# One decoder layer on one core: the feed-forward weights made ternary during the self-attention, and the first cross-attention inputs fetched there

## The reference

```
x = x + self_attention(layernorm(x))      # 16 heads of 128, window of 128, rope, sink, grouped output in two matrices
x = x + cross_attention(layernorm(x))     # 16 query heads of 32, 4 key/value heads, 1024 context rows a batch
x = x + feed_forward(layernorm(x))
```

```python
def weight_quant(w):
    scale = 1.0 / jnp.clip(jnp.mean(jnp.abs(w)), EPS)
    return jnp.clip(jnp.round(w * scale), -1.0, 1.0) / scale
gate = bitlinear(x, w_gate); up = bitlinear(x, w_up)
intermediate = jax.nn.silu(gate) * up
return h_bitlinear(intermediate, w_down)   # a Walsh-Hadamard transform over 2048 before the rounding
```

## Time and profile before

| | |
|---|---|
| time before, median of 3 runs | 1869.34 us (1868.5 to 1874.75) |
| the profiled execution, its own time | 1871.28 us |
| its span in the trace | 1869.4 us |
| mean granted TensorE clock | 0.968 of full speed |
| busy share of the span | PE 89%, DVE 62%, ACT 65%, POOL 63% |
| self-attention, steps | from about 88 to 659 us |
| cross-attention | from 659 to 1494 us |
| feed-forward | from 1494 us to the end |

### The profile page before, as it was taken

One profiled execution on the slowest core, in us unless ns is written; L12 is line 12 of the kernel. 1 busy time (PEld: TensorE's weight loads), 2 busy tenths in 40 slices (PEclk: granted clock), 3 DMA queues, 4 the chain that ended last, 5 costly groups with the idle time before them and its releaser, 6 DMA issues. The chain is left out here.

```text
span 1869.4 us, 24714 instructions
## 1 busy us (share of the span) xinstructions
PE 1663.9 (89%) x8118; PEld 1161.0 (62%) x8118; DVE 1163.6 (62%) x1997; ACT 1213.6 (65%) x1979; POOL 1177.1 (63%) x1080
## 2 busy tenths in 40 slices
PE   6999999999999958999999999999999606999996
PEld 3588888888888735556555655566656302666664
DVE  2366666666766536666855576556757266677764
ACT  2366666656665524887876687667869344788775
POOL 0478777877877503675755576556757306888892
PEclk9999999999999978999999999999999958999999
DMA  6100000000000055112210311120100080010000
GB/s 215 46 12 12 13 20 16 12 12 24 12 7 12 6 171 138 31 26 76 57 43 26 88 31 40 32 49 18 43 23 23 29 315 0 12 35 27 31 18 24
DMA packets 47103, 85.40 MB, mean 46 GB/s; under 512 B 7548, under 2 KB 12028, under 8 KB 45952
## 3 DMA queue, kind: packets, MB, share of 16 engines
q1 hardware_dynamic: 45136, 82.67, 14.3%
q10 hardware_dynamic: 1840, 1.14, 0.2%
HBM read 52.26 MB, written 12.58 MB: 35 GB/s over the span
## 5 line engine op out<-in xcount | busy, mean ns | idle before, releaser
L1146 POOL TENSOR_TENSOR x_p_lo<-x_p,x_p_hi 128x1024 fp32r<-128x1024 f32 x192 | 455.4, 2384 | 300.2 <-ACT x_p_hi L980 299.5
L1095 DVE TENSOR_REDUCE x_maxes<-x_ps_a 128x1 f32<-128x1024 f32 x256 | 313.1, 1223 | 258.1 <-PE x_ps_a L1229 257.2
L958 ACT ACTIVATE x_p<-x_ps_b,x_any_valid 128x1024 f32<-128x1024 f32 x256 | 284.9, 1113 | 168.5 <-PE x_ps_b L1217 167.8
L1217 PE MATMUL x_ps_b<-x_Q,x_K 100*128 100x512 f32 x512 | 228.1, 526 | 3.7 <-ACT x_p L958 2.2
L980 ACT ACTIVATE x_p_hi<-x_p 128x1024 fp32r<-128x1024 f32 x192 | 203.1, 1058 | 4.8
L1229 PE MATMUL x_ps_a<-x_K,x_Q 99*128 99x512 f32 x512 | 166.3, 406 | 6.8 <-DMA x_Q<-x_p_lo 3.9
L1255 PE MATMUL x_ps_o<-x_p_hi,x_V 128*96 128x512 f32 x384 | 157.1, 409 | 1.2 <-POOL x_p_lo L1146 1.2
L1256 PE MATMUL x_ps_o<-x_p_lo,x_V 128*96 128x512 f32 x384 | 150.9, 393 | 0.0
L1217 PEld LDWEIGHTS x_ps_b<-x_Q,x_K 100*128 100x128 f32 x512 | 90.1, 191 | 97.3 <-issue 76.1
L331 ACT ACTIVATE a_work<-a_ps_s,a_neg_max,a_q_r 128x256 f32<-128x256 f32 (+1 forms) x256 | 134.0, 538 | 4.7 <-DVE a_neg_max L419 4.7
L1260 PE MATMUL x_ps_o<-x_p,x_V 128*96 128x512 f32 x256 | 120.4, 591 | 0.0
(11 more groups left out here) (256 smaller groups left out, 4300.9 us busy)
## 6 DMA issues: line engine op xcount, KB each, us to landing
a_w_raw<-in_L_attn_out_w SPq DMA_DIRECT2D x8, 1024.0 KB, 7.8
x_ctxT<-in_ctx SPq DMA_DIRECT2D x8, 1024.0 KB, 7.3
x_Q<-x_q_hi SPq DMA_DIRECT2D x104, 64.0 KB, 2.0
a_xt<-in_x SPq DMA_DIRECT2D x16, 256.0 KB, 2.8
x_scratch<-a_work SPq DMA_DIRECT2D x16, 256.0 KB, 2.0
x_xt<-x_scratch SPq DMA_DIRECT2D x16, 256.0 KB, 3.6
x_K<-x_k_hi SPq DMA_DIRECT2D x32, 128.0 KB, 2.3
x_x1t<-x_scratch SPq DMA_DIRECT2D x16, 256.0 KB, 3.0
```

The lines of the kernel that those rows point to most:

```text
L958: act.activation(p[:, r, :, :], ps_b[:, :, :], ACT.Exp, scale=any_valid[:, b % 2:b % 2 + 1]).then_inc(exp_ready, 1)
L1095: dve.tensor_reduce(out=maxes[:, h2, r, 3:4], in_=ps_a[:, :, :], axis=mybir.AxisListType.XY, op=ALU.max)\
L1146: pool.tensor_tensor(out=p_lo[:, r], in0=p[:, r], in1=p_hi[:, r].bitcast(F32), op=ALU.subtract).then_inc(lo_ready, 1)
L1217: last = pe.matmul(ps_b[:, j, :], K[0:ROWS + 4, g, kb * P:(kb + 1) * P], Q[0:ROWS + 4, hh, :], start=True, stop=True)
```

## The change

The rounding of the three feed-forward weights leaves the feed-forward. It is done in the self-attention, in 24 chunks of 128 x 1024 (8 for each weight), in two passes over the fp32 weights in DRAM:

- Steps c = 0 to 23: SP loads a chunk into one of four slots, and DVE sums its magnitudes (a `tensor_reduce` of 128 x 1024, placed between L437 and L439). After 8 chunks DVE adds up (steps 8, 16, 24); SP writes 128 sums to DRAM, waits, and loads them back to all partitions; DVE adds them and makes mean and reciprocal (steps 11, 19, 27).
- Steps c = 14 to 37: the chunk is loaded again; ACT rounds it (`Copy` with a scale, before the wait of L316) and clips it from one side as bf16 (`Relu`, between the four `Exp` and the sink's); in the next step DVE clips the other side (a `tensor_scalar` of bf16, 128 x 1024, ahead of L380); SP stores the chunk to `ffn_quant` in DRAM. The weights are stored with the opposite sign, and four scale factors change sign.
- A buffer `shared` of 128 x 9216 fp32 outlives the phases. It holds the raw output matrices first, then the chunks, from c = 42 on the context, `wk`, `wq`, `wv`, and from c = 57 the first four tiles of x1. The cross-attention does not load these any more.
- In the last batch of the cross-attention SP loads gate and up as bf16 (2 MB each) from `ffn_quant` over the context and query weights. Down is loaded at the start of the feed-forward, behind two tiles of x2. The feed-forward begins with a `Silu` of 128 x 1.

```diff
+            def load_abs(k):
+                if k == 0:
+                    sp.wait_ge(w12_made, H1)
+                if k >= 4:
+                    sp.wait_ge(f_part_ready, k - 3)
+                sp.dma_start(chunk_view(f_abs[:, k % 4, :], k), ffn_source(k)).then_inc(f_abs_in[k % 4], 16)
+            def load_raw(k):
+                if k >= 2:
+                    sp.wait_ge(f_clip_ready, k - 1)
+                sp.dma_start(chunk_view(f_raw[:, k % 2, :], k), ffn_source(k)).then_inc(f_raw_in[k % 2], 16)
+            def store_quant(k):
+                sp.wait_ge(f_quant_ready, k + 1)
+                sp.dma_start(ffn_quant[k // 8, :, k % 8 * 1024:(k % 8 + 1) * 1024], f_quant[:, k % 2, :]).then_inc(f_stored[k % 2], 16)
...
+            for c in range(STEPS + 3):
+                if c + 2 < FFN_CHUNKS:
+                    load_abs(c + 2)
+                if 0 <= c - 16 < FFN_CHUNKS:
+                    store_quant(c - 16)
+                if 0 <= c - 12 < FFN_CHUNKS:
+                    load_raw(c - 12)
+                if c in (9, 17, 25):
+                    exchange_sums(c // 8 - 1)
...
# ACT, in step c, ahead of qT_hi
+                if 0 <= c - 14 < FFN_CHUNKS:
+                    k = c - 14
+                    act.wait_ge(f_raw_in[k % 2], 16 * (k // 2 + 1))
+                    act.wait_ge(f_scale_ready, k // 8 + 1)
+                    act.activation(f_raw[:, k % 2, :], f_raw[:, k % 2, :], ACT.Copy, scale=f_scale[:, k // 8:k // 8 + 1], bias=MAGIC)\
# ACT, between the four Exp and the sink's
+                        act.activation(f_quant[:, k % 2, :], f_raw[:, k % 2, :], ACT.Relu, scale=-1.0, bias=f_clip[:, :])\
# DVE, in step c, ahead of aT_lo
+                if 0 <= c - 15 < FFN_CHUNKS:
+                    k = c - 15
+                    dve.wait_ge(f_clip_ready, k + 1)
+                    dve.tensor_scalar(f_quant[:, k % 2, :], f_quant[:, k % 2, :], 2.0, 1.0, ALU.min, ALU.subtract).then_inc(f_quant_ready, 1)
# DVE, between q_eps and neg_r
+                    if 0 <= c < FFN_CHUNKS:
+                        dve.wait_ge(f_abs_in[c % 4], 16 * (c // 4 + 1))
+                        dve.tensor_reduce(out=f_part[:, c:c + 1], in_=f_abs[:, c % 4, :], axis=AXX, op=ALU.add,
+                                          apply_absolute_value=True).then_inc(f_part_ready, 1)
...
# SP, end of the cross-attention
+            for m, job in enumerate((("V", 1, B - 1), ("Q", 3, B - 1))):
+                sp.wait_ge(job_read, jobs_until(*job))
+                sp.dma_start(shared[:, m * 4096:(m + 1) * 4096].bitcast(BF16), ffn_quant[m]).then_inc(ffn_in[m], 16)
# PE, feed-forward
-                    weight_total(0)
-                    weight_total(1)
-                    pe.wait_ge(w_ready, 4)
+                    pe.wait_ge(ffn_in[0], 16)
+                    pe.wait_ge(ffn_in[1], 16)
```

More of the change, by code:

```diff
@@ L33 @@
 QSCALE = 32 ** -0.5
+F = 2048
+FFN_CHUNKS = 24
+MAGIC = 1.5 * 2.0 ** 23
+EPS_Q = 1e-5
 BIG = 1e30
-class At:
-    def __init__(self, c, b, per, total, looped):
-        self.c, self.b, self.per, self.total, self.looped = c, b, per, total, looped
-    def has(self, d):
-        return self.looped or 0 <= self.c + d < self.total
-    def after(self, d, first):
-        return self.looped or self.c + d >= first
-    def val(self, static, per):
-        return static + per * self.b if self.looped else static
-def hold(eng, sem, value, passed):
-    eng.wait_ge(sem, value)
-    eng.sem_inc(passed, 1)
 def clear_semaphores(nc, sems):
@@ L64, in clear_semaphores, with __init__, sem, early @@
         nc.gpsimd.sem_clear(s)
+class CrossFetch:
+    def __init__(self, nc, stack, shared, ctx_t, wq, wk, wv):
+        def sem(name):
+            return stack.enter_context(nc.semaphore("x_" + name))
+        self.sources = ctx_t, wq, wk, wv
+        self.ctxT = shared[:, 0:4096].rearrange("p (j c n) -> p j c n", j=2, c=DC)
+        self.wq = shared[:, 4096:6144].rearrange("p (c n) -> p c n", c=DC)
+        self.wk = shared[:, 6144:6656].rearrange("p (c n) -> p c n", c=DC)
+        self.wv = shared[:, 6656:7168].rearrange("p (c n) -> p c n", c=DC)
+        self.xt = shared[:, 7168:9216].rearrange("p (i n) -> p i n", i=TPB)
+        self.wk_in, self.wv_in, self.wq_in = sem("wk_in"), sem("wv_in"), sem("wq_in")
+        self.ctx_in = [sem(f"ctx_in{j}") for j in range(2)]
+        self.x1_in = [sem(f"x1_in{j}") for j in range(TPB)]
+        self.sems = [self.wk_in, self.wv_in, self.wq_in] + self.ctx_in + self.x1_in
+    def early(self, sp):
+        ctx_t, wq, wk, wv = self.sources
+        sp.dma_start(self.wk, wk.rearrange("(c p) n -> p c n", p=P)).then_inc(self.wk_in, 16)
+        for j in range(2):
+            sp.dma_start(self.ctxT[:, j], ctx_t[0, :, j * 512:(j + 1) * 512].rearrange("(c p) n -> p c n", p=P)).then_inc(self.ctx_in[j], 16)
+        sp.dma_start(self.wq, wq.rearrange("(c p) n -> p c n", p=P)).then_inc(self.wq_in, 16)
+        sp.dma_start(self.wv, wv.rearrange("(c p) n -> p c n", p=P)).then_inc(self.wv_in, 16)
+    def late(self, sp, x1_rows):
+        for i in range(TPB):
+            sp.dma_start(self.xt[:, i, :], x1_rows[i * P:(i + 1) * P, :]).then_inc(self.x1_in[i], 16)
 def decoder_layer(nc, ins, out):
@@ new lines, in _ @@
+            load_abs(0)
+            load_abs(1)
+            for c in range(STEPS + 3):
[7 more added lines that the diff above has]
+                    exchange_sums(c // 8 - 1)
+                if c == 42:
+                    for j in range(2):
+                        sp.wait_ge(f_stored[j], 16 * (FFN_CHUNKS // 2))
+                    sp.wait_ge(f_part_ready, FFN_CHUNKS)
+                    fetch.early(sp)
+                if c == 57:
+                    sp.wait_ge(qckT_made, TILES)
+                    fetch.late(sp, x1_rows)
+                if c % 4 == 2 and 0 <= (c - 6) // 4 < TILES:
+                    t = (c - 6) // 4
+                    sp.wait_ge(x1_ready, t + 1)
+                    sp.dma_start(x1_rows[t * P:(t + 1) * P, :], x1[:, t % 2, :]).then_inc(x1_stored[t % 2], 16)
+                    if t + XR1 < TILES:
+                        load_x(t + XR1)
@@ L707, in phase_cross_attention @@
         const_in, maxes_in = sem("const_in"), sem("maxes_in")
-        wk_in, wv_in, wq_in, wo_in, mask_in = (sem(n) for n in ("wk_in", "wv_in", "wq_in", "wo_in", "mask_in"))
-        ctx_in = [sem(f"ctx_in{j}") for j in range(2)]
-        x1_in = [sem(f"x1_in{j}") for j in range(TPB)]
+        wk_in, wv_in, wq_in, ctx_in, x1_in = fetch.wk_in, fetch.wv_in, fetch.wq_in, fetch.ctx_in, fetch.x1_in
+        wo_in, mask_in = sem("wo_in"), sem("mask_in")
         res_in = [sem(f"res_in{j}") for j in range(3)]
```

242 lines of the change are left out of this document (99 added, 143 removed).

## The result

The changed kernel takes 1842.11 us, the median of 4 runs (1841.13 to 1846.15), against 1869.7 us: a ratio of 0.985, with a 95% interval of 0.983 to 0.988. It was forecast at 1827 us, with 1815 to 1845 as the range. So it gained 27.6 us where 42 were forecast. The profiled execution took 1846.15 us (span 1844.3), 4 us above the median; before it was 1.9 above.

What follows compares the result with a forecast made beforehand. TensorE was taken to bound the kernel except at the cross-attention's and feed-forward's starts. Self-attention +6, cross-attention −1 and feed-forward −47 gave −42 us: 1827 us against the median, range 1815 to 1845 for 8 in 10.

Steps and rivals of the forecast that it cites:

- the likeliest case: Whole kernel: all terms as forecast, 1815 (gain 51, self-attention +1, constants −2) to 1836 us (gain 44, +12); chance 0.68.
- only the wait for the weights gained: Feed-forward start: first quarters no quicker, so the two gains of 5.7 us are missing; about 1839 us, chance 0.13.
- GpSimd first at the port: Self-attention: DVE loses the port in all 24 steps, costing 36 us in place of 6; about 1857 us, chance 0.12.
- the wait for a DMA ahead of an ACT pass: Sign of being wrong: a DMA wait standing ahead of an ACT pass, the first gate product or the down product.
- sign of being right: Self-attention: its end moves by 4 to 9 us, in the steps with c % 4 = 0.
- The wait for the weights: Feed-forward start: first gate product waits for the first tile alone, at 1506.1 rather than 1540.9; gain 34.8 us.
- The quarters and halves: Feed-forward start: GpSimd's first pair of quarters, then first pair of halves, come sooner without the rounding; gain 5.7 us each.
- The constants: Feed-forward start: `f_ident_bf` waited 4.80 us for a transfer sharing queues with 12 MB of weights; gain taken as 1 us.
- SP's transfers: Self-attention: chunk transfers of 512 KB, asked for two steps of 8.2 us ahead, are hidden; cost 0.
- The clip: Self-attention, DVE behind L442: meets GpSimd's L494 at the port; costs 1.5 to 7.2 us with c % 4 = 0, 1.2 with 3.
- ScalarE's cover: Self-attention: ACT's rounding (1.14 us) and `Relu` (1.15) hide in waits of 1.38 and 1.29 us; the second barely.
- the rival on the other side: Self-attention: the two ACT passes are not hidden, 55 us against 48 gained; about 1882 us, chance 0.04.

## Why the prediction was right, and where it was wrong

- **The time was within the range, in part by luck.** The measured 1842.11 us lies outside the range of the likeliest case itself, 1815 to 1836 (its lower end should read 1817 by its own terms: 1869.3 − 51 + 1 − 2). The range reached 1845 to take in two rivals, only the wait for the weights gained and GpSimd first at the port, and neither happened; the stalls that came instead were in no term and no rival. One of the prediction's own signs of being wrong came true, the wait for a DMA ahead of an ACT pass, and the self-attention's steps grew by 18.9 us, where 4 to 9 were its sign of being right.
- **The feed-forward was right.** 47 us were forecast and 46.65 measured up to the last result. The wait for the weights, 34.8, came out to the tenth. That the sum did so too is partly chance, since three terms were off and cancel. The quarters and halves gained 7.3 and 7.7, not 5.7 each: I had counted products at 1.9 us throughout, and from the second quarter's gate product on, at 1532.01, they took 1.15 us or less. The constants came no earlier (4.73 us of wait ahead of `f_ident_bf`, 4.80 before), where 1 was forecast. And 3.3 came back by the last result, 2.2 of it in the last two tiles. There the last 16 down products took 5.53 us, and 3.61 before. The granted clock was 0.62 in 9 us around them, and 0.79 in 8 us around those of before:

```profile
1829.00:1838.00 9.00, 7.26 (x27) 2.90 (x25) 1.70 (x3) 2.19 (x3) 0.00 (x0) 0.62 0.08 30
```

```profile
1854.00:1862.00 8.00, 6.81 (x36) 3.24 (x36) 1.66 (x3) 3.50 (x4) 0.00 (x0) 0.79 0.09 35
```

- **The step that failed is "SP's transfers ... Hidden: 0. The small exchanges and sums at six steps: 0.7 us together."** I priced the loads, which are asked for two steps ahead, and not the store that frees one of only two slots, nor what stands ahead of it on SyncE: a wait of 8.4 us for 512 bytes. That stores are queued behind this wait could be read from the code; how long such a write takes, no row of before showed. It cost 15.2 to 18.1 us in steps 13 to 38 (237.50 to 240.44 in three executions, against 222.34 without the exchange), and 17 by the medians with four slots. Four slots (1825.46) and no exchange (1822.38) both show what remains without it, and both are within 5 us of the 1827 that was forecast.
- **The clip was oversized.** The self-attention's term was 3.4 to 9.1, taken as 6; the clips make up 2.7 to 8.4 of it. With the stalls gone, all of the added work costs 1.0 us in steps 13 to 38, and leaving the clips out gives 1.4 back. The order in which they issue was as read: ahead of GpSimd with c % 4 = 1 and 2, 0.82 us behind with 3, and a tie with 0, which VectorE wins by 0.06 us every time. What the port rival builds on is seen: where the clip comes second, it stands until GpSimd is through. The Trainium skill ("SBUF — State Buffer", section "Who interferes with whom") states this rule; the runs agree, with 1.35 and 0.42 us for the two orders. The rival's price, 1.5 us a step and 36 in all, was never reached: it comes second in the six steps with c % 4 = 3 and costs 0.95 us there in all (1.2 were forecast), and one place later all 24 clips cost 16.7 us, and they themselves are only 5.6 us longer. What 24 clips right behind the reciprocal but second at the port would cost, no run shows.
- **ScalarE's cover held**, as forecast, and the rival on the other side, that both passes are exposed, is answered: at the sink's `Exp` there is less than one more pass of room, ahead of the queries there is room for nearly a whole one.
- **The cross-attention was right about the fetch and wrong about the sign.** The cast does come first and the loads were hidden. But the constants landed 2.4 us later, not 1 earlier, because the 1 MB of output weights had moved ahead of them; with its load behind the constants the cast comes after 3.7 us.
- The 1.5 us between the last reciprocal and the cross-attention are TensorE's clock. TensorE waits there 2.0 us for the normalisation. In 8 of the 13 profiled executions it then works for some 4 us partly at the lower of its two levels (1.2 GHz; a granted clock of 0.66 on the mean of 5 us), and the stretch takes 16.8 us; in the other 5 it stays at 2.4 GHz (1.00), and the stretch takes 15.3. Which it is does not follow what was changed. The first row is of before, the second of after:

```profile
645.00:657.00 12.00, 8.35 (x38) 6.31 (x38) 3.14 (x4) 1.63 (x2) 1.12 (x1) 1.00 0.00 0
```

```profile
664.00:669.00 5.00, 4.86 (x19) 4.00 (x20) 1.22 (x1) 1.02 (x1) 0.09 (x1) 0.66 0.00 0
```

What decides which of the two an execution gets is open.

## What to carry to other kernels

When work is put into the waits of a loop, look at the transfers that free its buffers as closely as at the passes: count the slots, and go through what the issuing queue does ahead of each store, its waits above all. A round trip of a few bytes through DRAM is no small thing for a queue that waits for it, nor for a large store that runs beside it; here two more slots gave 17 us, and the better order of the queue only 6 (both by the medians). And when loads are moved out of a start, the ones that stay move ahead of the small constants on which everything waits.

## What the runs showed of the hardware

Writing 128 values of 4 bytes, one from each partition, to 512 bytes of DRAM kept SyncE waiting 8.4 us (issue 240.93, next issue 249.34), and a store of 256 KB beside it landed in 10.5 us from the same queue and in 10.4 from the other, where such stores land in 2.0 to 6.0 us in the kernel without it. Why so few bytes hold so long was not tried. A second thing is that an order of two engines that is decided by 0.06 us came out the same in all six steps of each of the ten kernels in which the clip stands in that place.
